# An audio encoder layer on one core: keys and queries projected transposed from folded float32 weights, score products summed by TensorE transposes, LayerNorm's scale put into the scores

## The chip, the cores and the metric

The kernel runs on one core of a Trainium2 chip. The metric is the time of one execution on the device in microseconds. The program is one launch; five engines (TensorE or PE, VectorE or DVE, ScalarE or ACT, GpSimd or POOL, and SyncE or SP, which here issues nearly all DMAs) each run their own instruction stream in the order in which it is written, and wait for one another by semaphores.

## The reference

```python
patches = x[:, idx, :].reshape(B, n, 128)          # B = 64 series, n = 10 overlapping patches
h = einsum('bnp,dp->bnd', patches, W) + b          # 640 tokens, d = 512
# attention over axis 0 of "b, s": 16 heads of 32, rotary positions, causal
q, k, v = ln(h) @ Wq.T, ln(h) @ Wk.T, ln(h) @ Wv.T
q, k = rope(q, k)
scores = q . k / sqrt(32), causal
heavy = top_k(sum over queries of softmax(scores), int(0.1 * 10))   # one key for each head
scores = where(heavy | (|i - j| <= 1), scores, -max)
h = h + (softmax(scores) . v) @ Wo.T
gate, up = split(ln(h) @ w_gate_up.T)              # 2 * 2048
h = h + (silu(gate) * up) @ w_down.T
```

`ln` is LayerNorm without weights. Each of the 64 series has 10 positions, so attention is 10 x 10 for each series and head.

## The kernel before

**Tokens.** The 640 tokens lie in five tiles of 128. A tile holds four positions of 32 series (`QUADRANTS`): tiles 0 and 1 are positions 0 to 7 of group 0 (the first 32 series), tiles 3 and 4 those of group 1, and tile 2 has positions 8 and 9 of both. Matrix products run in float32r with each operand split into a high and a low part, so each product is three matmuls (`mm3`). ACT makes the high parts; DVE or POOL the low ones, by subtraction.

**Front, group 0.** `embed` makes h for five tiles on PE; DVE takes LayerNorm's statistics, POOL the power, DVE `normalise`; PE transposes the result, and `project` makes keys, queries and values, 15 tiles of 12 matmuls. DVE turns keys and queries (`rotate`: three operations on PSUM), POOL adds the two halves (`rotation_sum`). SP writes each tile of k, q and v to a scratch tensor `regroup` in HBM (`leave`, four DMAs) and reads it back (`enter`), so that a partition holds one quarter of the heads of one series: `k_all`, `q_all`, `v_all`. Scores of query i are then one product over its i + 1 keys (`key_products`, L236) and one sum over the 32 channels of a head (L707), both on a partition's own 128 channels; POOL does some of the products (`POOL_SCORES`, `POOL_VALUES`). Softmax (`softmax_in`, `exponential` on ACT, `softmax_out`) runs twice: once to find the heavy key (`heavy_keys`), once with the mask. `value_products` (L240) multiply values by probabilities; PE sums them over keys and transposes them at once by real matmuls with an identity (`value_sums`, L1014). Then `project_out`, the second LayerNorm, and its transposes.

**First pass, tiles 0 and 1.** The feed-forward network goes over 16 blocks of weights, streamed from HBM into four slots of `stage`. For each block PE does `gate_up` (24 matmuls of 256 columns) and `down` of the block before (6 of 512); ACT does the silu and the high parts; DVE `up_product` (L847) and `low_product` (L853); POOL the low parts of the weights (`lo_gu`, `lo_down`, L364). Between the blocks' operations, in an order written out by hand, DVE does all of group 1's attention, since tiles 2 to 4 need it. PE's `value_sums` of group 1 stand after block 11, and `project_out` of tiles 2, 4 and 3 among blocks 12 to 15.

**Second pass, tiles 2 to 4.** The same 16 blocks again, 384 columns wide, with no attention beside it.

## Time and profile before

| | us |
|---|---|
| timed runs (3), median | 328.0 (327.45 to 328.83) |
| the profiled execution, its own time | 324.37 |
| its span, first to last instruction | 322.6 |
| PE busy | 278.0 |
| DVE busy | 209.8 |
| POOL busy | 157.7 |
| ACT busy | 112.0 |

Busy times are sums over stages with different limits. The profiled execution took 3.6 us less than the median of the timed runs; 1.8 us of its time lie outside the span. The granted TensorE clock was 0.973 of full speed in the mean.

### The profile page before, as it was taken

The numbers are of one execution on the slowest core, as the hardware profiler recorded it, in microseconds if no ns is written. First come the engines' busy times: TensorE is split into PE (matmuls) and PEld (weight loads), VectorE is DVE, ScalarE is ACT, GpSimd is POOL, SyncE is SP. The second block draws the span as 40 slices with busy tenths as digits, with TensorE's granted clock in tenths as the row PEclk, the third lists the DMA queues.
The fourth block names the chain that finished last, engine by engine and source line by source line (L and its number), as shares of the span: only waits on it lengthen the run. The fifth ranks groups of instructions, "written<-read, shape, count | busy, mean of one in ns | idle before, by whom it ended". The sixth has DMA issues, their size and how long they took to land.

```text
span 322.6 us, 4390 instructions
## 1 busy us (share of the span) xinstructions
PE 278.0 (86%) x1528; PEld 244.4 (76%) x1528; DVE 209.8 (65%) x307; ACT 112.0 (35%) x185; POOL 157.7 (49%) x107
## 2 busy tenths in 40 slices
PE   2989769969495799849757999899999999999994
PEld 1558648849385798749647998789999999999993
DVE  3687999999959998768499634676342333234213
ACT  4561101035101444562722223253443343344320
POOL 0565795109679598765399404542233223222310
PEclk9999989997999899998979999999999999999999
DMA  7903787504554053524320500252732442340003
GB/s 251 408 6 67 177 280 172 188 17 120 151 139 163 2 189 106 195 98 139 142 108 0 197 0 0 100 192 63 272 127 98 145 148 98 108 162 23 0 0 98
DMA packets 17902, 39.89 MB, mean 124 GB/s; under 512 B 2208, under 2 KB 10656, under 8 KB 17376
## 3 DMA queue, kind: packets, MB, share of 16 engines
q1 hardware_dynamic: 17600, 39.32, 37.8%
q10 hardware_dynamic: 288, 0.39, 0.3%
q8 instruction: 7, 0.11, 0.1%
q14 instruction: 7, 0.06, 0.1%
HBM read 34.46 MB, written 5.24 MB: 123 GB/s over the span
## 4 chain that ended last, share of the span: by engine, by line
PE 49%; DVE 28%; issue 9%; ACT 5%; POOL 3%; DMA 3%; SPq 2%; DVEq 0%; ACTq 0%; POOLq 0%
PE ps L201 41%; DVE prod L236 5%; PE ps L1014 4%; DVE hT L853 3%; DVE sm L707 3%; SPq L274 2%; POOL wvo L364 2%; DVE pr L735 2%; DVE gu L847 2%; DMA bias_raw<-b_tok 1%; DVE xn L670 1%; DVE prod L240 1%; DVE xT L677 1%; DVE rstd L667 1%; DVE rowv L725 1%
## 5 line engine op out<-in xcount | busy, mean ns | idle before, releaser
L201 PE MATMUL ps<-xT,wgu 128*128 128x256 f32 (+1 forms) x768 | 121.2, 314 | 1.9 <-DVE xT L677 1.8
L201 PEld LDWEIGHTS ps<-xT,wgu 128*128 128x128 f32 x768 | 118.1, 192 | 5.3 <-DVE xT L677 2.5
L364 POOL TENSOR_TENSOR wd<-stage,wd 128x512 fp32r<-128x512 f32 x32 | 51.6, 1613 | 80.1 <-ACT wd L477 80.1
L201 PE MATMUL ps<-wd,hT 128*128 128x512 f32 x240 | 64.0, 409 | 15.2 <-DVE hT L853 13.6
L201 PEld LDWEIGHTS ps<-wd,hT 128*128 128x128 f32 x240 | 45.3, 195 | 25.2 <-DVE hT L853 15.0
L847 DVE TENSOR_TENSOR gu<-silu,ps 128x256 f32<-128x256 f32 (+1 forms) x32 | 15.5, 484 | 62.1 <-PE ps L201 44.9
L364 POOL TENSOR_TENSOR wgu<-stage,wgu 128x1024 fp32r<-128x1024 f32 x16 | 40.1, 2505 | 12.3 <-ACT wgu L477 12.3
L477 ACT ACTIVATE wgu<-stage 128x1024 fp32r<-128x1024 f32 x32 | 33.8, 1055 | 22.1 <-PE ps L201 22.1
L853 DVE TENSOR_TENSOR hT<-gu,hT 128x256 fp32r<-128x256 f32 (+1 forms) x32 | 24.3, 759 | 19.8 <-ACT hT L477 19.8
L201 PE MATMUL ps<-wvo,xT 128*128 128x512 f32 x120 | 31.0, 412 | 5.7 <-issue 3.2
L201 PEld LDWEIGHTS ps<-wvo,xT 128*128 128x128 f32 x120 | 23.2, 197 | 11.8 <-POOL wvo L364 3.4
L1014 PE MATMUL ps<-const,prod 128*128 128x128 f32 x220 | 27.6, 287 | 5.1 <-DVE prod L240 5.1
L1014 PEld LDWEIGHTS ps<-const,prod 128*128 128x128 f32 x220 | 27.0, 202 | 6.2 <-issue 5.4
L578 ACT ACTIVATE silu<-ps 128x256 f32<-128x256 f32 (+1 forms) x32 | 13.9, 436 | 47.6 <-PE ps L201 47.6
L477 ACT ACTIVATE xT<-ps 128x512 fp32r<-128x512 f32 (+1 forms) x16 | 9.1, 571 | 53.4 <-PE ps L1014 26.7
L477 ACT ACTIVATE hT<-gu 128x256 fp32r<-128x256 f32 (+1 forms) x32 | 14.8, 462 | 35.8 <-DVE gu L847 35.7
L240 DVE TENSOR_TENSOR prod<-v_all,pr 128x896 f32<-128x896 f32 (+8 forms) x15 | 25.9, 1765 | 0.1
L477 ACT ACTIVATE wd<-stage 128x512 fp32r<-128x512 f32 x32 | 20.0, 625 | 8.5 <-PE ps L201 8.5
L236 DVE TENSOR_TENSOR prod<-q_all,k_all 128x128 f32<-128x128 f32 (+7 forms) x15 | 21.5, 1434 | 0.0
L387 POOL TENSOR_TENSOR rot<-rot_cos,rot_sin 128x512 f32<-128x512 f32 x10 | 12.8, 1284 | 17.5 <-DVE rot_sin L698 17.5
L838 DVE TENSOR_TENSOR wgu<-stage,wgu 128x1024 fp32r<-128x1024 f32 x16 | 19.7, 1234 | 1.0 <-ACT wgu L477 1.0
L707 DVE TENSOR_REDUCE sm<-prod 128x4 f32<-128x128 f32 (+9 forms) x20 | 17.5, 885 | 0.5
(76 smaller groups left out, 257.4 us busy)
## 6 DMA issues: line engine op xcount, KB each, us to landing
stage<-w_ffn SPq DMA_DIRECT2D x32, 768.0 KB, 4.3
regroup<-rot SPq DMA_DIRECT2D x40, 64.0 KB, 2.5
regroup<-v_out SPq DMA_DIRECT2D x20, 64.0 KB, 2.0
stage<-w_k SPq DMA_DIRECT2D x1, 1024.0 KB, 6.4
stage<-w_q SPq DMA_DIRECT2D x1, 1024.0 KB, 8.9
stage<-w_v SPq DMA_DIRECT2D x1, 1024.0 KB, 10.9
stage<-w_o SPq DMA_DIRECT2D x1, 1024.0 KB, 12.9
k_all<-regroup SPq DMA_DIRECT2D x4, 256.0 KB, 2.7
```

The source lines that it names most:

```text
L201: ins = pe.matmul(dst, lhs[a], rhs[b], start=first and n == 0, stop=last and n == 2)
L236: return eng.tensor_tensor(products(i), repeated(q_all[:, g, i], 1, i + 1), k_all[:, g, 0:i + 1], ALU.mult)
L240: return eng.tensor_tensor(products(i).rearrange("p j (h d) -> p j h d", d=HD), v_all[:, g, 0:i + 1].rearrange("p j (h d) -> p j h d", d=H ...
L364: pool.tensor_tensor(dst, src, f32(hi), ALU.subtract).then_inc(done, 1)
L387: pool.tensor_tensor(rot[:, n % ROT], rot_cos[:, n % 2], rot_sin[:, n % 2], ALU.add).then_inc(rot_sum, 1)
L477: act.activation(dst, src, ACT.Copy).then_inc(done, 1)
L578: act.activation(silu[:, ring, cols], ps[:, gate, at:at + P * TILES[p]], ACT.Silu).then_inc(silu_done[p], 1)
L707: dve.tensor_reduce(sm[:, i, :, 0:i + 1].rearrange("p h j -> p j h"), products(i).rearrange("p j (h d) -> p j h d", d=HD), AX_X, ALU.add). ...
L838: dve.tensor_tensor(wgu[:, ring, 1], stage[:, slot, 0:2 * KT * P], f32(wgu[:, ring, 0]), ALU.subtract)\
L847: dve.tensor_tensor(gu[:, ring, cols], silu[:, ring, cols], ps[:, up, at:at + P * TILES[p]], ALU.mult)\
L853: dve.tensor_tensor(hT[:, ring, 1, cols], gu[:, ring, cols], f32(hT[:, ring, 0, cols]), ALU.subtract).then_inc(hT_lo[p], 1)
L1014: ins = pe.matmul(dst, products(i)[:, j], cut["ident"], start=j == 0, stop=j == i)
```

## The change

**Keys and queries.** LayerNorm subtracts a mean and multiplies by one number for each token. The mean is taken out of the embedding's weights (`token_mean`, `tok_mid`), and these are multiplied with Wk and Wq on PE (`fold_matrix`, and `fold_column` for the embedding's bias). So keys and queries without LayerNorm's scale are one float32 matmul of the raw patches (`project`), and come out transposed: channels in partitions, tokens along the row. Their four chunks of 128 channels are ordered so that a rotation is between chunks. They need no trip through HBM. LayerNorm's scale of the query's and of the key's token are multiplied into the scores instead (`scales` on POOL, `scale_tables` and `scaled` on DVE).

**Scores.** `products` makes, for four positions of queries at once (128 lanes wide, two positions: 64), the products with all of 4, 8 or 10 keys, causal or not, in four operations for each `ii`. `score_sums` transposes each 128 x 128 piece on PE and adds the four chunks in PSUM, by matmuls in transpose mode; `reduced` adds the last eight of 32 channels. A partition now holds a query's position and series, and a row 3 x 16 x 10 scores. `key_totals` on PE adds the first softmax over queries and positions.

**Values.** Wv is folded likewise (`fold_matrix`, `fold_bias`, `value_tile`), the result scaled by LayerNorm's scale on ACT, and still goes through HBM, now with four DMAs of 32 partitions for `enter`. `values` multiplies two keys at a time, 1024 elements in each operation; `value_sums` sums and transposes by transpose mode. POOL does no products any more.

**Other.** 16 matmuls on constant data stand at PE's start; the output is added into `h` in place.

The core of the diff:

```diff
+            def leave(t):
+
+                sp.wait_ge(v_sb, t + 1)
                 for q, (g, i) in enumerate(QUADRANTS[t]):
...
+                    sp.dma_start(regroup[g, :, i, :], v_out[GB * q:GB * (q + 1), t % 2]).then_inc(v_gone[t % 2], 16)
+
+            def enter(g, at):
+
+                for q in range(NQ):
+                    sp.dma_start(v_all[GB * q:GB * (q + 1), at, :], regroup[g, :, at, :]).then_inc(dma_v[g], 16)
...
+            def value_in(g, t):
+                sp.wait_ge(v_gone[t % 2], 16 * NQ * (t // 2 + 1))
+                places = [i for group, i in QUADRANTS[t] if group == g]
+                enter(g, slice(places[0], places[-1] + 1))
...
+            for t in range(NT):
+                leave(t)
+                if 1 <= t <= 3:
+                    value_in(0, t - 1)
+            sp.wait_ge(fold_mm, 6)
...
+            def rotation_sum(n, pair):
+
+                g, x = PROJECT[n]
+                pool.wait_ge(rot_read, KT * n + 2 * pair + 2)
+                at = CHUNKS[2 * pair]
+                chunks = slice(at, at + 3, 2)
+                pool.tensor_tensor(kq[g][x][:, chunks], by_cos[:, chunks], by_sin[:, chunks], ALU.add).then_inc(rot_sum, 1)
...
+            for n in range(2):
+                for pair in range(2):
+                    rotation_sum(n, pair)
...
+            scales()
             for k in range(KT):
...
+                lo_wo(k)
+            for n in range(2, 4):
+                for pair in range(2):
+                    rotation_sum(n, pair)
...
             def values_out(t):
 
-                n = PROJECT.index(("v", t))
-                act.wait_ge(project_mm, n + 1)
+                act.wait_ge(value_mm, t + 1)
+                act.wait_ge(rstd_set, 1)
                 if t >= 2:
-                    act.wait_ge(v_gone[t % 2], 64 * (t // 2))
-                act.activation(v_out[:, t % 2], ps[:, PROJECT_BANK[n % len(PROJECT_BANK)], :], ACT.Copy).then_inc(v_sb, 1)
+                    act.wait_ge(v_gone[t % 2], 16 * NQ * (t // 2))
+                act.activation(v_out[:, t % 2], ps[:, VALUE_BANK[t], :], ACT.Copy, scale=h_rstd[:, t:t + 1]).then_inc(v_sb, 1)
...
+            for t in range(NT):
                 values_out(t)
             exponential(0)
+            for t in range(2):
+                act.wait_ge(v_gone[1 - t], 16 * NQ * (2 + t))
+            act.wait_ge(score_mm, len(PIECES) // 2)
+            hi_gu(A, 0, 0, 0)
             exponential(1)
             exponential(2)
-            for t in range(NT - 2, NT):
...
+            def lo_row():
+                dve.wait_ge(fold_out, 6)
+                rows = slice(BR, 2 * BR)
+                dve.tensor_tensor(fold_row[rows], ps[rows, FOLD_BANK["v", "row"], :], f32(fold_row[rows]), ALU.subtract)\
+                   .then_inc(fold_lo, 1)
...
+            def rotate(n, pair):
+
+                g, x = PROJECT[n]
+                dve.wait_ge(fold_out, 2 + 2 * "kq".index(x))
+                if n:
+                    dve.wait_ge(rot_sum, 2 * n + pair - 1)
+                for at in (2 * pair, 2 * pair + 1):
...
+                    dve.scalar_tensor_tensor(by_cos[:, c].rearrange("p (i b) -> p i b", b=GB), src, own, repeated(cos, 2, GB),
+                                             ALU.add, ALU.mult)
+                    dve.scalar_tensor_tensor(by_sin[:, (c + 2) % KT].rearrange("p (i b) -> p i b", b=GB), src, own,
+                                             repeated(sin, 2, GB), ALU.add, ALU.mult).then_inc(rot_read, 1)
...
+            def products(g, ii):
+
+                k, q = kq[g]["k"], kq[g]["q"]
+                if g:
+                    dve.wait_ge(pv_mm, 3)
+                n, at = KEYS[ii], P * ii
+                wide = WIDTH[ii] // GB
+                for place, c in enumerate(CHUNKS):
+                    dve.wait_ge(rot_sum, 4 * g + 2 + place // 2 + 1)
+                    query = q[:, c, at:at + WIDTH[ii]].rearrange("p (q b) -> p q b", b=GB)
+                    key = k[:, c, 0:GB * n].rearrange("p (j b) -> p j b", b=GB)
+                    dve.tensor_tensor(sprod[ii][:, :, c].rearrange("p j (q b) -> p j q b", b=GB),
+                                      repeated(query, 1, n), repeated(key, 2, wide), ALU.mult).then_inc(score_prod, 1)
...
+                for n, bank in enumerate(SCORE_BANK[g, ii]):
+                    dve.wait_ge(score_mm, PIECES.index((g, ii, n)) + 1)
+                    m = min(4, KEYS[ii] - 4 * n)
+                    dve.tensor_reduce(sr[0:WIDTH[ii], ii, :, 4 * n:4 * n + m].rearrange("p h j -> p j h"),
+                                      ps[0:WIDTH[ii], bank, 0:P * m].rearrange("p (j h f) -> p j h f", j=m, h=H),
+                                      AX_X, ALU.add).then_inc(score_sum, 1)
...
+                dve.wait_ge(score_sum, len(PIECES) // 2 * (g + 1))
+                step(dve.tensor_tensor(sm[:, :, :, :], sr[:, :, :, :], repeated(rr[:, g], 2, H), ALU.mult))
+                step(dve.tensor_tensor(sm[:, :, :, :], sm[:, :, :, :],
+                                       repeated(cut["causal"].rearrange("p (i j) -> p i j", j=NPOS), 2, H), ALU.min))
...
+            def heavy_keys(g):
+
+                dve.wait_ge(heavy_mm, g + 1)
+                total = ps[:, HEAVY_BANK[g], 0:H * NPOS].rearrange("p (h j) -> p h j", h=H)
+                step(dve.tensor_reduce(hvm[:, 0], total, AX_X, ALU.max))
...
+                    dve.tensor_tensor(vprod[ii][rows, j:j + PAIR].rearrange("p j (h d) -> p j h d", d=HD),
+                                      v_all[rows, j:j + PAIR].rearrange("p j (h d) -> p j h d", d=HD),
+                                      repeated(pr[rows, ii, :, j:j + PAIR].rearrange("p h j -> p j h"), 3, HD), ALU.mult)\
+                       .then_inc(pv_prod, 1)
...
+            products(0, 2)
+            lo_fold()
+            products(0, 1)
+            products(0, 0)
+            reduced(0, 2)
+            reduced(0, 1)
+            scale_tables()
+            reduced(0, 0)
             softmax_in(0)
-            rotate("k", 3)
+            lo_row()
             softmax_out(0)
-            heavy_keys()
+            rotate(2, 0)
+            heavy_keys(0)
             softmax_in(1)
             softmax_in(2)
+            rotate(2, 1)
             softmax_out(1)
-            values(0, 7, 6)
+            values(0)
             softmax_out(2)
-            values(0, 5, 4, 3, 2, 1, 0)
-            rotate("q", 3)
-            rotate("k", 4)
-            rotate("q", 4)
+            values(1)
+            values(2)
+            rotate(3, 0)
+            rotate(3, 1)
...
+            reduced(1, 2)
             first_pass(3)
-            scores(1, 9)
+            reduced(1, 1)
+            reduced(1, 0)
             first_pass(4)
             softmax_in(3)
             first_pass(5)
             up_product(A, 6, 0)
             softmax_out(3)
             low_product(A, 6, 0)
-            heavy_keys()
             first_pass(7)
+            heavy_keys(1)
...
-            values(1, 9)
+            values(3, 0, 6)
             up_product(A, 10, 0)
-            values(1, 6)
+            values(3, 6)
             low_product(A, 10, 0)
-            values(1, 5, 3)
+            values(4)
             up_product(A, 11, 1)
-            values(1, 2, 1)
             low_product(A, 11, 1)
-            values(1, 0)
+            values(5)
...
+                for k in range(KT):
+                    ins = pe.matmul(ps[:, FOLD_BANK[x, "matrix"], :], tok_mid[:, k, 0:P], weights(x, k),
+                                    start=k == 0, stop=k == KT - 1)
+                ins.then_inc(fold_mm, 1)
...
+                    dst, weight = ps[:, PROJECT_BANK[g, x][c], :], fold[x][:, P * c:P * (c + 1)]
+                    if g == 0:
...
+            def score_sums(g, ii, lasts):
+
+                pe.wait_ge(score_prod, KT * (SCORES.index((g, ii)) + 1))
+                rows = WIDTH[ii]
+                for n, bank in enumerate(SCORE_BANK[g, ii]):
+                    read_out(*lasts[n])
+                    m = min(4, KEYS[ii] - 4 * n)
+                    for j in range(m):
+                        for c in range(KT):
+                            ins = pe.matmul(ps[0:rows, bank, P * j:P * (j + 1)], sprod[ii][:, 4 * n + j, c], cut["ident"],
+                                            is_transpose=True, start=c == 0, stop=c == KT - 1)
+                    ins.then_inc(score_mm, 1)
...
+                    rows = slice(0, WIDTH[ii])
+                    ins = pe.matmul(ps[:, HEAVY_BANK[g], 0:H * NPOS], cut["batch"][rows],
+                                    pr[rows, ii].rearrange("p h j -> p (h j)"), start=ii == 0, stop=ii == NI - 1)
+                ins.then_inc(heavy_mm, 1)
...
-                    for j in range(i + 1):
-                        ins = pe.matmul(dst, products(i)[:, j], cut["ident"], start=j == 0, stop=j == i)
-                    ins.then_inc(pv_mm, 1)
+                rows, n = WIDTH[ii], KEYS[ii]
+                for j in range(n):
+                    if j % PAIR == 0:
+                        pe.wait_ge(pv_prod, VALUES.index((u, j)) + 1)
+                    for k in range(KT):
+                        ins = pe.matmul(ps[:, UNIT_BANK[u], P * k + GB * a:P * k + GB * b], vprod[ii][0:rows, j, P * k:P * (k + 1)],
+                                        cut["ident"][0:rows, 0:rows], is_transpose=True, start=j == 0 and k == 0,
+                                        stop=j == n - 1 and k == KT - 1)
+                ins.then_inc(pv_mm, 1)
...
+            score_sums(1, 2, [("unit", 2), ("rotation", ((1, "q"), 2)), ("rotation", ((1, "q"), 1))])
+            first_pass(2, 0)
+            score_sums(1, 1, [("rotation", ((1, "q"), 3)), ("score", (1, 2, 0))])
+            first_pass(3, 1)
+            score_sums(1, 0, [("score", (1, 2, 1))])
+            for i in range(4, 7):
+                first_pass(i, i % 2)
+            key_totals(1, ("score", (1, 2, 2)))
+            for i in range(7, 12):
+                first_pass(i, i % 2)
+
```

In ACT's order, at the end of group 0's front, before (`v_out<-ps` is `values_out`, `pr<-pr` an exponential, `wgu<-stage` the first block's high part, `wvo<-stage` the high part of Wo):

```order
L507 ACTIVATE v_out<-ps 128x512 x3
L512 ACTIVATE pr<-pr 128x400
L512 ACTIVATE pr<-pr 128x320
L512 ACTIVATE pr<-pr 128x80
L507 ACTIVATE v_out<-ps 128x512 x2
L477 ACTIVATE wvo<-stage 128x512 x4
L477 ACTIVATE wgu<-stage 128x1024
L477 ACTIVATE wd<-stage 128x512
```

and now, from the last embedding tile on (`fold_row<-ps` is the folded bias of the values):

```order
L451 ACTIVATE fold_v<-ps 128x512
L438 ACTIVATE v_out,h_square<-h,h_neg 128x512 x5
L429 ACTIVATE wo<-stage 128x512 x4
L451 ACTIVATE fold_row<-ps 64x512
L465 ACTIVATE v_out<-ps,h_rstd 128x512 x5
L470 ACTIVATE pr<-pr 128x480
L429 ACTIVATE wgu<-stage 128x1024
L470 ACTIVATE pr<-pr 128x320
L470 ACTIVATE pr<-pr 128x160
L429 ACTIVATE wd<-stage 128x512
```

The first exponential stood after three `values_out`; it now stands after all five, and the second one after the split of the first feed-forward block.

On DVE, around the first softmax of group 0, now (`sr` are the sums of score products, `rr` the scale table, `fold_row` the low part that `value_tile` waits for):

```order
L684 TENSOR_REDUCE sr<-ps 128x4x16
L691 TENSOR_TENSOR sm<-sr,rr 128x480
L692 TENSOR_TENSOR sm<-sm,const 128x480
L722 TENSOR_REDUCE rowv<-sm 128x48
L723 TENSOR_SCALAR rowv<-rowv 128x48
L724 SCALAR_TENSOR_TENSOR pr<-sm,rowv 128x480
L612 TENSOR_TENSOR fold_row<-ps,fold_row 32x512
L731 TENSOR_REDUCE rowv<-pr 128x48
L732 RECIPROCAL rowv<-rowv 128x48
L733 TENSOR_TENSOR pr<-pr,rowv 128x480
L660 SCALAR_TENSOR_TENSOR by_cos<-ps,column,const 128x320
L662 SCALAR_TENSOR_TENSOR by_sin<-ps,column,const 128x320
```

The low part of the folded bias (L612) stands behind the whole of the first `softmax_in`, and `softmax_out` (L731 to L733) behind that, before the rotation of group 1's keys.

On PE, in the first pass, before (`xT,wgu` is `gate_up`, `wd,hT` is `down`; rows L1051 to L1085 are a loop over ten blocks):

```order
L201 MATMUL ps<-xT,wgu 128x256 x48
L201 MATMUL ps<-wd,hT 128x512 x6
L1085 UNCONDITIONAL_BRANCH
L1085 ISA
L1051 REGISTER_ALU
L201 MATMUL ps<-xT,wgu 128x256 x24
L1064 REGISTER_ALU
L201 MATMUL ps<-wd,hT 128x512 x6
L1051 REGISTER_ALU
L201 MATMUL ps<-xT,wgu 128x256 x24
```

and now, from block 0 to the first block after the key totals (`sprod` are score products, `pr,const` is `key_totals`):

```order
L232 MATMUL ps<-wd,hT 128x512 x6
L1040 MATMUL ps<-const,sprod 64x128 x40
L232 MATMUL ps<-xT,wgu 128x256 x24
L232 MATMUL ps<-wd,hT 128x512 x6
L1040 MATMUL ps<-const,sprod 128x128 x32
L232 MATMUL ps<-xT,wgu 128x256 x24
L232 MATMUL ps<-wd,hT 128x512 x6
L1040 MATMUL ps<-const,sprod 128x128 x16
...
L232 MATMUL ps<-wd,hT 128x512 x6
L1057 MATMUL ps<-pr,const 128x160 x3
L232 MATMUL ps<-xT,wgu 128x256 x24
L232 MATMUL ps<-wd,hT 128x512 x6
```

Three stretches of transposes and one of `key_totals` have been put between the blocks; each stands ahead of a `gate_up`.

## Rows read from the trace of the kernel before

**Rows 1.** The page: the span, and busy us, share and instructions of PE.

```profile
span 322.6 us, 4390 instructions
PE 278.0 (86%) x1528; PEld 244.4 (76%) x1528; DVE 209.8 (65%) x307; ACT 112.0 (35%) x185; POOL 157.7 (49%) x107
```

**Rows 2.** Windows: stretch, length, busy us of each engine, PE clock, DMA share, GB/s.

```profile
28.00:60.80 32.80, 28.46 (x118) 22.20 (x117) 31.09 (x47) 2.99 (x5) 20.96 (x16) 0.95 0.71 190
60.80:87.50 26.70, 19.22 (x110) 16.64 (x108) 25.61 (x49) 9.41 (x16) 14.06 (x9) 0.94 0.41 113
102.50:184.40 81.90, 66.52 (x445) 61.33 (x445) 69.21 (x73) 33.23 (x55) 59.43 (x28) 0.94 0.34 119
184.40:215.60 31.20, 29.76 (x191) 25.97 (x190) 16.90 (x34) 10.04 (x19) 11.02 (x11) 1.00 0.18 65
215.60:322.60 107.00, 102.72 (x534) 95.81 (x534) 39.05 (x53) 40.61 (x64) 26.48 (x16) 1.00 0.31 105
```

**Rows 3.** The chain that ended last: start us, us, what.

```profile
174.56 10.05 PE ps L1014 x90
...
196.65 0.44 PE ps L983 x4
...
215.58 102.07 PE ps L201 x531
```

**Rows 4.** Timeline of the embedding tiles on PE, at either clock.

```profile
9.27 0.63 PE L954 MATMUL ps<-wtok,pat 128*128 128x512 f32 x1
9.69 0.63 PE L956 MATMUL ps<-wtok,pat 128*128 128x512 f32 x1
...
15.67 0.48 PE L952 MATMUL ps<-wtok,pat 128*128 128x512 f32 x1
...
16.55 0.50 PE L958 MATMUL ps<-bias,share 64*128 64x512 f32 x1
```

**Rows 5.** Timeline of PE's weight loads: the four loads of one tile's transposes.

```profile
213.13 0.42 PEld L983 LDWEIGHTS ps<-const,xn 128*128 128x128 f32 x4 [0.29 <-DVE xn L670]
```

**Rows 6.** Timeline of DVE in the first pass, and two groups by shape.

```profile
106.74 0.68 DVE L236 TENSOR_TENSOR prod<-q_all,k_all 128x512 f32<-128x512 f32 x1
107.46 0.69 DVE L707 TENSOR_REDUCE sm<-prod 128x16 f32<-128x512 f32 x1
...
108.39 0.82 DVE L236 TENSOR_TENSOR prod<-q_all,k_all 128x640 f32<-128x640 f32 x1
...
L240 DVE TENSOR_TENSOR prod<-v_all,pr 128x1024 f32<-128x1024 f32 x1 | 1.2, 1225 | 0.1
...
L698 DVE TENSOR_TENSOR rot_sin<-ps,const 128x256 f32<-128x256 f32 x20 | 7.4, 413 | 0.0
```

**Rows 7.** Timeline of SP's queue: two value tiles leave and one comes back.

```profile
70.78 1.77 SPq L274 DMA_DIRECT2D regroup<-v_out  x4
73.89 0.34 SPq L282 DMA_DIRECT2D v_all<-regroup  x1
74.27 1.89 SPq L274 DMA_DIRECT2D regroup<-v_out  x4
77.85 0.34 SPq L282 DMA_DIRECT2D v_all<-regroup  x1
```

**Rows 8.** Timeline of ACT: the first exponential, a value tile, an exponential in the first pass.

```profile
52.71 0.60 ACT L507 ACTIVATE v_out<-ps 128x512 f32<-128x512 f32 x1 [2.13 <-PE ps L201]
60.85 0.54 ACT L512 ACTIVATE pr<-pr 128x400 f32<-128x400 f32 x1 [7.54 <-DVE pr L726]
```

**Rows 9.** Timeline: a product on DVE, and POOL's operation beside it.

```profile
113.17 3.28 DVE L236 TENSOR_TENSOR prod<-q_all,k_all 128x896 f32<-128x896 f32 x1
...
112.82 2.68 POOL L364 TENSOR_TENSOR wgu<-stage,wgu 128x1024 fp32r<-128x1024 f32 x1
```

**Rows 10.** Groups by line on POOL: busy us, mean ns, idle before.

```profile
L364 POOL TENSOR_TENSOR wgu<-stage,wgu 128x1024 fp32r<-128x1024 f32 x16 | 40.1, 2505 | 12.3 <-ACT wgu L477 12.3
...
L240 POOL TENSOR_TENSOR prod<-v_all,pr 128x1152 f32<-128x1152 f32 (+3 forms) x5 | 12.9, 2586 | 0.0
...
L236 POOL TENSOR_TENSOR prod<-q_all,k_all 128x768 f32<-128x768 f32 (+2 forms) x5 | 12.7, 2561 | 2.4 <-DMA q_all<-regroup 2.4
```

782 lines of the change are left out of this document (369 added, 413 removed).

## The prediction

> **What bounds the kernel now.** I read the page, then the windows by stage, then the chain of waits and the timelines. PE is busy 278.0 of 322.6 us [rows 1], but the windows show that it is the limit in two stages only: 102.7 of 107.0 us in the second pass, and 29.8 of 31.2 us at the end of the first [rows 2]. The chain agrees: one piece of 102.07 us on PE to the end [rows 3]. The change does not touch the second pass. In the other stages DVE is the busiest: 31.1 of 32.8 us before the first softmax of group 0 is ready (28.0 to 60.8), 25.6 of 26.7 us from there to the first `low_attn` (87.5), and 69.2 of 81.9 us from the start of the first pass (102.5) to the end of group 1's value sums (184.4) [rows 2]. So the change is worth what it does to DVE's order in these three stretches, and to what DVE waits for.
>
> DVE's time in the first pass is not all its own. A product of 896 elements took 3.28 us, with POOL in an operation of 2.68 us when it came up [rows 9], where 640 elements undisturbed took 0.82 [rows 6]. A DVE operation takes about 0.15 us and 1.05 ns per element: 512 took 0.68 or 0.69, 640 took 0.82, 1024 took 1.225 [rows 6]. By that rule the stretch 102.5 to 184.4 holds 6.7 us of products (8, of 5248 elements), 8.9 of sums (10, of 7040), 5.5 of value products (7, of 4224), 24 operations of 256 elements for the blocks (0.41 each, 9.9) and some 9.4 for softmaxes, masks and heavy keys: 40.4 us. The other 28.8 of 69.2 are waits for POOL inside the operations.
>
> **The front until the first softmax is ready (60.8 now).** PE leads here. A float32 matmul goes as two instructions; 90 of 128 columns took 10.05 us [rows 3], so one takes 0.223 us, 0.89 at 512 columns and 0.56 at 320. `fold_matrix` is 4 x 0.89 = 3.6, `project` 4 x 0.56 = 2.2. `fold_column` has 16 matmuls of one column, 32 weight loads; the loads of a transposed tile come 0.1 us apart, four in 0.42 [rows 5], so at least 3.3; at most 0.3 for each of 32, 9. I take 4, near the loads. The 16 matmuls on constants and the mean end at about 8, on the low clock: 512 columns in 0.42 us there [rows 4], 1.2 GHz, so 16 x 0.45 = 7.1. Then k: 8 + 3.6 + 4 + 2.2 = 17.8, q the same: 27.6. Five embedding tiles at 1.3 us (15.67 to about 17.0 [rows 4]) 34.1, `fold_matrix` of v 37.7, copy and `lo_fold` 39.0. DVE, which has rotated and made `products(0, 2)` by 33, stands before `lo_fold`, so `products(0, 1)` (4 x 1.15, as the next starts before the last has ended) and `(0, 0)` (4 x 0.6) end at 46.1; sums 2.8, scale tables 1.4, the last sum 0.6, scaling 1.3, `softmax_in` 1.5: 53.7, with 2 us for POOL's split of Wo beside it 55.7. Term A: 55.7 - 60.8 = **-5 us** (between -10 and +5, the latter with the columns at 9 us).
>
> **The first exponential.** Now it starts at 60.85, released by its input from DVE [rows 8]. In the new order ACT does it behind `values_out(4)`, and that chain starts only when DVE has made `lo_row`, 0.7 us after `softmax_in(0)`. Call that L. Value tile and ACT's copy of 0.60 us [rows 8] end at L + 1. Four DMAs leave, issue 1.8 us; from the first issue to the next read 3.1 and 3.6 us pass [rows 7]. So tile 0 has landed at L + 4.2, `values_out(2)` ends at L + 4.9. SP has meanwhile sent tile 1 (to L + 4.6), and then issues the four new DMAs of `value_in` (0.43 each, to 6.4), then tile 2: issue to 8.2, landed 9.6. `values_out(4)` ends at 10.3, the exponential at L + 11. Behind it wait `softmax_out`, PE's key totals, the mask and everything later on DVE; nothing covers it. Before, two rotations did. Term B: 0.7 + 11 = **+12 us** (9 to 14). What is late next is the second exponential, behind `leave(4)` and the block's split: L + 18, but its input comes at L + 19, so that wait is nearly covered.
>
> **The rest of group 0 on DVE.** `softmax_out` 1.9, rotations of group 1 in 16 operations of 320 elements on PSUM at 0.4 (256 took 0.41 [rows 6], so 0.4 from start to start) 6.6, heavy keys 2.3, two masked `softmax_in` 4.0, `softmax_out` 2.4, and `values` 11 operations of 1024 elements, 12.7: 29.9, against 26.7 now [rows 2]. Term C: **+3 us** (-1 to +6). From `low_attn(0)` to the first `gate_up`, 15 us, I change nothing: the same `project_out`, LayerNorm and POOL's `lo_gu` stand there.
>
> **Group 1 in the first pass.** By the same rule DVE's own work becomes 10.9 us of products (12, of 8704 elements, since non-causal pairs are made too), 3.9 of sums, 13.4 of value products (11 x 1.225), 9.9 for the blocks and 11.3 for softmaxes of 480 elements and two scaling operations: 49.4, +9. POOL loses its products, 12.7 and 12.9 us in the whole kernel [rows 10], about 10 of the 59.4 us in this stretch [rows 2]; if the waits shrink in proportion, 28.8 becomes 24, -5. New waits: `key_totals(1)` needs `softmax_out(3)` and stands ahead of `gate_up` 7, which thereby follows it (24 x 0.112 = 2.7 us, and the totals 0.8) instead of lying beside it; `score_sums` of 32 and 16 transposes (0.1 each) stand ahead of `gate_up` 3 and 4, which DVE's next blocks need. I take +6. Term D: **+10 us**. Bounds: +4 if only the first two count; +22 if each POOL operation of the stretch meets a DVE product, which is what laying the blocks out one after another gives.
>
> At the end of the pass `value_sums(5)` has 16 transposes for 20 matmul instructions, -0.4; the rest stays.
>
> The Trainium skill ("SBUF — State Buffer", on the shared port pair) says that a DVE operation with two SBUF inputs and a GpSimd operation hold one port pair exclusively, so that the loser fully blocks. The trace agrees [rows 9]. By it alone the stretch would be set by the sum of both engines' port work; POOL's loss and DVE's gain nearly cancel, and D would be about +4.
>
> **Sum.** -5 + 12 + 3 + 10 = +20 us on the profiled execution's 324.4, so 344.4. The timed median lay 3.6 us above that execution, so 348.
>
> **Rivals.** (1) The exponential is not held: the value round trip ends sooner, or the wait is covered. Then B is 2, the rest as above: 338. Against it: the order of ACT's rows, and 3.1 us for each trip [rows 7]. (2) Faster: POOL's work, no longer doubled by products, falls into DVE's waits and reductions, and the waits inside DVE's operations in the first pass shrink from 28.8 to 5 us. Then D is 9 - 24 + 6 = -9, or -15 without new waits, and with A at its lower bound of -10 the sum is -10 + 12 + 3 - 15 = -10: 318. It decides when those waits fall under some 12 us. For it: products of 512 and 640 elements in the first pass ran undisturbed [rows 6]; against it: POOL keeps its 2.5 us of `lo_gu` for each block [rows 10], and DVE's two-input work grows. (3) The clock. Group 1's and group 0's sums are long stretches of transposes now. The windows show 0.94 in the first pass and 1.00 in the stretch with 90 real matmuls in a row [rows 2, 3]; no run here shows a long stretch of transposes. If they leave PE on the low clock, 72 transposes and the `project_out` and block behind them, 7 us at full clock, take some 6 us more in the PE-bound end, and the front 3: 357. The Trainium skill ("TensorE: Matmul & The Clock Gate", Part 4) says that transpose mode does not count as busy for the clock. That speaks for this case; the trace has only four transposes at a time.
>
> **How the numbers follow.** Likeliest: slower by about 20, terms as above, 0.55, own range 338 to 358. Rival 1 (still slower) 0.12. Rival 3 0.14. Rival 2, faster, 0.13; the small remainder lies around no change. What this measurement can tell from no change is about 0.5%, 1.6 us. Faster 0.14, same 0.04, slower 0.82. The range must leave out no more than 0.2: the faster case and a little above; 331 to 362.
>
> **What would show it.** In the changed profile: first softmax input on DVE near 56; ACT's first exponential with an idle DVE of some 11 us before `softmax_out`; first `gate_up` near 113; `project_out` of tile 2 near 204; the last stretch of PE unchanged at 102 us. I am wrong if the exponential starts within 2 us of its input, if the DVE products in the first pass run at 1.2 us with POOL busy beside them, or if the folds on PE take half of what I gave them.

## The result, and the profile after

The changed kernel took 368.8 us (median of 4 runs, 368.28 to 369.72), the one before 327.7 beside it: 1.125 times the time, interval 1.121 to 1.130. The prediction, 348 us with a range of 331 to 362, had the direction right and the size at half. The profiled execution has a span of 367.9 us against 322.6 [rows 1], 45.3 more. That is some 4 us more than the medians differ (41.0): the profiled execution of the kernel before lay 3.4 us under its median, that of the changed kernel 1.0 above. Of the runs below, executions at a lower granted clock are left out, one of ten of `all_together` (378.7 us) and two of four of `all_pieces_128` (344.6 and 340.4 us). The page of the changed kernel:

```profile
span 367.9 us, 4574 instructions
PE 301.1 (82%) x1678; PEld 259.3 (70%) x1678; DVE 206.3 (56%) x293; ACT 110.4 (30%) x189; POOL 125.9 (34%) x85
...
PEclk9887999955859699699569898999999999999999
```

DVE has fewer instructions and less busy time than before [rows 1], POOL 32 us less. PE's granted clock has digits of 5 and 6 in the front and the first pass. I cut both spans at the same five events, to see where 45.3 us went:

| from, to | before | after | grew by | predicted |
|---|---|---|---|---|
| start, first `softmax_out` | 61.99 | 75.10 | 13.1 | A + B = 7 |
| `softmax_out(0)`, `low_attn(0)` | 25.5 | 31.6 | 6.1 | C = 3 |
| `low_attn(0)`, first `gate_up` | 15.1 | 17.3 | 2.1 | 0 |
| first `gate_up`, `project_out(2)` | 81.7 | 108.3 | 26.6 | D = 10 |
| `project_out(2)`, end | 138.2 | 135.6 | -2.6 | -0.4 |

The last stage became 2.6 us shorter; 0.4 of that was in the sum, the rest is not explained. The timeline of DVE, around the first exponential:

```profile
59.42 0.66 DVE L724 SCALAR_TENSOR_TENSOR pr<-sm,rowv 128x480 f32<-128x480 f32 x1
60.11 0.68 DVE L612 TENSOR_TENSOR fold_row<-ps,fold_row 32x512 fp32r<-32x512 f32 x1
75.10 0.65 DVE L731 TENSOR_REDUCE rowv<-pr 128x48 f32<-128x480 f32 x1 [14.31 <-ACT pr L470]
```

and of ACT, which answers to [rows 8]:

```profile
62.70 0.69 ACT L465 ACTIVATE v_out<-ps,h_rstd 128x512 f32<-128x512 f32 x1 [0.63 <-PE ps L1029]
65.22 0.69 ACT L465 ACTIVATE v_out<-ps,h_rstd 128x512 f32<-128x512 f32 x1 [1.84 <-DMA regroup<-v_out]
67.11 0.69 ACT L465 ACTIVATE v_out<-ps,h_rstd 128x512 f32<-128x512 f32 x1 [1.20 <-DMA regroup<-v_out]
73.89 0.69 ACT L465 ACTIVATE v_out<-ps,h_rstd 128x512 f32<-128x512 f32 x1 [6.10 <-DMA regroup<-v_out]
74.48 0.59 ACT L470 ACTIVATE pr<-pr 128x480 f32<-128x480 f32 x1
```

The exponential's input is complete at 60.08; ACT runs it at 74.48, behind five copies, the last of which waited 6.10 us for its buffer. DVE stands 14.31 us. The clock and PE's waits in the first pass are in this timeline of PE:

```profile
149.64 3.67 PE L1040 MATMUL ps<-const,sprod 128*128 128x128 f32 x16 [3.83 <-DVE sr L684]
152.97 4.20 PE L232 MATMUL ps<-xT,wgu 128*128 128x256 f32 x24
...
160.04 3.10 PE L232 MATMUL ps<-xT,wgu 128*128 128x256 f32 x24
...
182.25 2.23 PE L1057 MATMUL ps<-pr,const 128*128 128x160 f32 x6 [5.88 <-DVE pr L733]
184.41 5.42 PE L232 MATMUL ps<-xT,wgu 128*128 128x256 f32 x24
```

Two pieces of attention work in PE's order (a piece of `score_sums(1, 1)`, and `key_totals(1)`) wait 3.83 and 5.88 us, and a block's 24 matmuls behind them take 4.20 and 5.42 us, against 3.1 at full clock.

### The profile page after: what moved, and what is told of

Its sections match the earlier page's. It is cut to its first block, busy times and chain, and to the rows that moved or that the text cites. A ratio compares the mean times of both kernels' runs of the same rounds, so it can differ in the third digit from the quotient of the medians.

```text
span 367.9 us, 4574 instructions
## 1 busy us (share of the span) xinstructions
PE 301.1 (82%) x1678; PEld 259.3 (70%) x1678; DVE 206.3 (56%) x293; ACT 110.4 (30%) x189; POOL 125.9 (34%) x85
## 4 chain that ended last, share of the span: by engine, by line
PE 59%; DVE 24%; issue 7%; ACT 4%; DMA 2%; SPq 1%; POOL 1%; ACTq 0%; DVEq 0%
PE ps L232 41%; DVE sprod L676 3%; DVE vprod L762 3%; PE ps L969 3%; PE ps L1040 3%; PE ps L1079 2%; PE ps L998 2%; PE ps L977 2%; DMA regroup<-v_out 2%; DVE pr L733 2%; DVE hT L831 2%; PE ps L1095 2%; PE ps L1057 1%; DVE sr L684 1%; SPq L266 1%
## 5 line engine op out<-in xcount | busy, mean ns | idle before, releaser
L329 POOL TENSOR_TENSOR wd<-stage,wd 128x512 fp32r<-128x512 f32 x32 | 57.1, 1786 | 85.0 <-ACT wd L429 85.0
L232 PE MATMUL ps<-wd,hT 128*128 128x512 f32 x240 | 63.7, 408 | 16.0 <-DVE hT L831 14.6
L762 DVE TENSOR_TENSOR vprod<-v_all,pr 128x1024 f32<-128x1024 f32 (+1 forms) x22 | 30.9, 1459 | 0.1
L676 DVE TENSOR_TENSOR sprod<-q,k 128x640 f32<-128x640 f32 (+2 forms) x24 | 28.8, 1263 | 0.0
L1040 PE MATMUL ps<-const,sprod 128*128 128x128 f32 (+1 forms) x176 | 22.2, 286 | 5.4 <-DVE sr L684 3.8
L1040 PEld LDWEIGHTS ps<-const,sprod 128*128 128x128 f32 (+1 forms) x176 | 20.9, 135 | 6.9 <-DVE sr L684 4.1
L232 PE MATMUL ps<-wo,xT 128*128 128x512 f32 x60 | 16.3, 428 | 11.3 <-issue 11.3
L232 PEld LDWEIGHTS ps<-wo,xT 128*128 128x128 f32 x60 | 12.3, 209 | 14.5 <-issue 11.8
L1079 PE MATMUL ps<-const,vprod 128*128 128x128 f32 (+1 forms) x176 | 18.4, 264 | 1.7 <-DVE vprod L762 1.7
L1079 PEld LDWEIGHTS ps<-const,vprod 128*128 128x128 f32 (+1 forms) x176 | 17.3, 149 | 3.5 <-issue 3.1
L429 ACT ACTIVATE xT<-ps 128x512 fp32r<-128x512 f32 (+1 forms) x11 | 6.2, 560 | 43.3 <-PE ps L1079 31.5
```

What stands on the lines that cost most here:

```text
L232: ins = pe.matmul(dst, lhs[a], rhs[b], start=first and n == 0, stop=last and n == 2)
L329: pool.tensor_tensor(dst, src, f32(hi), ALU.subtract).then_inc(done, 1)
L429: act.activation(dst, src, ACT.Copy).then_inc(done, 1)
L676: dve.tensor_tensor(sprod[ii][:, :, c].rearrange("p j (q b) -> p j q b", b=GB), repeated(query, 1, n), repeated(key, 2, wide), ALU.mult).t ...
L762: dve.tensor_tensor(vprod[ii][rows, j:j + PAIR].rearrange("p j (h d) -> p j h d", d=HD), v_all[rows, j:j + PAIR].rearrange("p j (h d) -> p ...
L1040: ins = pe.matmul(ps[0:rows, bank, P * j:P * (j + 1)], sprod[ii][:, 4 * n + j, c], cut["ident"], is_transpose=True, start=c == 0, stop=c = ...
```

## The experiments

All times are medians, each kernel measured beside the one before (327.5 to 328.0). The three kernels named `quiet` leave a part of the computation out.

| kernel | us | against what it edits |
|---|---|---|
| `exp0_first` | 365.0 | -3.8 |
| `exp_all_first` | 366.4 | -2.4 |
| `totals_later` | 361.6 | -7.2 |
| `sums_read_earlier` | 363.9 | -4.9 |
| `wide_column` | 365.1 | -3.7 |
| `four_edits` | 348.0 | -20.7 |
| `quiet_after` | 336.8 | -32.0 |
| `quiet_before` | 312.2 | -15.7 on before |
| `four_early_front` | 340.7 | -7.3 on `four_edits` |
| `four_pool_pieces` | 333.9 | -14.1 on `four_edits` |
| `quiet_four` | 322.8 | -25.3 on `four_edits` |
| `four_fillers` | 342.6 | -5.4 on `four_edits` |
| `pieces_after` | 355.9 | -12.9 |
| `pieces_before` | 317.8 | -9.7 on before |
| `all_together` | 327.8 | -40.9 |
| `all_pieces_128` | 332.3 | +4.5 on `all_together` |

**The held exponential (B).** On ACT:

```diff
+            exponential(0)
             for t in range(NT):
                 values_out(t)
-            exponential(0)
```

> The changed kernel (368.8 us) with one edit: on ACT exponential(0) stands ahead of the five values_out copies instead of behind them. Theory (the held exponential, term B): the scores' input to it is ready at 60.1 us, so it should run at about 60 and the wait of DVE of 14.3 us ahead of softmax_out(0) goes. Then the next hold shows: exponential(1) still stands behind hi_gu(A, 0), which waits for v_out's last copy, at 81.4; so I expect 3 to 6 us less, 363 to 366. Rival (the values' round trip through memory bounds it, the exponential only waits beside it): v_all's last piece lands at about 80 and the values' products start at once behind it, no more than 1 us less or nothing. A further reading: with PE's wait of 7 us at 70 gone, project(1, q) and value_sums should show a granted clock near 1.0 instead of 0.5.

It took 365.0 us (ratio 1.117, 1.107 to 1.127), in the first theory's range. The exponential runs at 59.38 and `softmax_out(0)` at 60.09, 15 us sooner, but the first `gate_up` comes at 118.79 against 124.00, only 5.2 sooner. The timeline of DVE in this kernel shows what stood behind the held exponential:

```profile
61.26 0.66 DVE L733 TENSOR_TENSOR pr<-pr,rowv 128x480 f32<-128x480 f32 x1
70.49 0.55 DVE L660 SCALAR_TENSOR_TENSOR by_cos<-ps,column,const 128x320 f32<-128x320 f32 x1 [8.57 <-PE ps L1001]
...
74.28 0.33 DVE L740 TENSOR_REDUCE hvm<-ps 128x16 f32<-128x160 f32 x1 [1.61 <-PE ps L1057]
```

DVE now waits for PE, where `project(1, k)` and `key_totals(0)` stand behind the five value tiles. In the timeline of PE in this kernel these follow one another without a gap, but slowly:

```profile
64.20 1.65 PE L232 MATMUL ps<-fold_v,pat 128*128 128x512 f32 x3
...
68.80 1.22 PE L1000 MATMUL ps<-pat_raw,fold_k 128*128 128x256 f32 x2
...
73.01 1.23 PE L1057 MATMUL ps<-pr,const 128*128 128x160 f32 x6
```

From the matmul that `lo_row` releases to the end of `project(1, k)` PE takes 13.06 us here, all busy, at a mean granted clock of 0.61, and 9.27 us at 1.00 in the changed kernel, where three matmuls of a value tile take 0.97 us. The hold was real, but it covered another one, made of PE's order and of the clock. The expected clock near 1.0 came only for a part: it was 0.84 from 70 to 80, but 0.50 from 62 to 70 and 0.55 from 80 to 90. So the second theory on ACT was tried too:

```diff
+            exponential(1)
+            exponential(2)
             for t in range(2):
                 act.wait_ge(v_gone[1 - t], 16 * NQ * (2 + t))
             act.wait_ge(score_mm, len(PIECES) // 2)
             hi_gu(A, 0, 0, 0)
-            exponential(1)
-            exponential(2)
```

> As exp0_first, and exponential(1) and exponential(2) also stand ahead of ACT's wait for v_out to have left and of hi_gu(A, 0). Theory (term B whole): everything from softmax_out(0) on moves by what heavy_keys(0) gains, about 8 us (79.4 to 71.4), until the values have not arrived: 8 to 12 us less than the changed kernel, 357 to 361, the upper end if the clock stays up as well. Rival: the arrival of the values stops it at 4 to 6 us, and the time is that of exp0_first.

366.4 us, 2.4 less than the changed kernel and no less than `exp0_first`: near the rival's total, but not for its reason. The values' products did not wait for their arrival; they start at 85.0 here and at 84.3 there. `softmax_out(1)` stands behind `rotate(2, 1)`, so an earlier exponential had nobody waiting for it. `four_early_front` edits PE's order (on top of `four_edits`, below), together with the moves on DVE and ACT that its expectation names; what each of them gave was not measured apart. On PE:

```diff
             value_tile(1, ("fold low", 1))
+            key_totals(0, ("score", (0, 0, 0)))
...
-            key_totals(0, ("score", (0, 0, 0)))
             project(1, "q", ...)
```

> four_edits (348.0 us) with the way of group 0 freed of the values' queue: on PE key_totals(0) stands behind value_tile(1) instead of behind project(1, k); on DVE heavy_keys(0) and softmax_in(1), (2) stand ahead of rotate(2, 0); on ACT exponential(1), (2) stand ahead of values_out(4). In four_edits heavy_keys(0) begins at 71.7 behind key_totals, which waits for the values and the projection ahead of it in PE's order, though the first softmax is out at 57.8. Theory (what was left of term B is PE's order): heavy_keys at about 60 and the values' products start when v_all has landed (its last pieces were issued at 69.0 and took 5.6), near 76 instead of 82: 4 to 7 us less, 341 to 344. Rival (project(1, k) and the rotations behind it bound the front): less than 2 us.

340.7 us, 7.3 less, a little more than expected. Heavy keys start at 60.6 instead of 71.7, the first value product at 75.92 instead of 81.74, without a wait for v_all, and the first `gate_up` at 110.04 instead of 116.16. In `all_together`, which has the same order, DVE waits 5.90 us ahead of its first value product for v_all's transfer (76.81): there the arrival of the values is the limit of the front.

**The two waits of PE in the first pass (D).** `key_totals(1)` behind the block instead of ahead of it:

```diff
             for i in range(4, 7):
                 first_pass(i, i % 2)
+            pe.wait_ge(gu_prod[A], 6)
+            gate_up(A, 7, 1)
             key_totals(1, ("score", (1, 2, 2)))
-            for i in range(7, 12):
+            down(A, 6, 0)
+            for i in range(8, 12):
                 first_pass(i, i % 2)
```

> The changed kernel with one edit: PE's key_totals(1) stands between gate_up(A, 7) and down(A, 6) instead of ahead of gate_up(A, 7). In the changed kernel PE waits 5.9 us ahead of key_totals(1) and then runs gate_up 7 at a granted clock of 0.53 in 5.4 us. Theory (these waits are on the path of the pass): 5 to 9 us less, 360 to 364. Rival (DVE is the bound of this stretch and the wait only moves): within 2 us of 368.8.

and DVE empties the scores' bank sooner:

```diff
             low_product(A, 1, 1)
+            reduced(1, 2)
             up_product(A, 2, 0)
             products(1, 0)
             low_product(A, 2, 0)
-            reduced(1, 2)
             first_pass(3)
```

> The changed kernel with one edit: on DVE reduced(1, 2), which empties the bank that the second piece of score_sums(1, 1) needs, stands ahead of up_product(2) and products(1, 0) instead of behind them. In the changed kernel PE waits 3.8 us there and gate_up 3 comes out at 157.3 instead of about 150. Theory (this bank's wait is part of the loss of the pass): 4 to 7 us less, 362 to 365. Rival (products on DVE bound the stretch, and what PE gains it waits for later): less than 2 us.

361.6 and 363.9 us: 7.2 and 4.9 less, both inside the first theory's range. In the timeline of PE of `totals_later` the wait has fallen to 1.74 us and the blocks beside it run at full clock:

```profile
177.20 3.22 PE L232 MATMUL ps<-xT,wgu 128*128 128x256 f32 x24
182.16 1.25 PE L1057 MATMUL ps<-pr,const 128*128 128x160 f32 x6 [1.74 <-DVE pr L733]
184.97 3.01 PE L232 MATMUL ps<-xT,wgu 128*128 128x256 f32 x24
```

In that of `sums_read_earlier` the 32 transposes of `score_sums(1, 1)` run in one piece:

```profile
144.72 3.68 PE L1040 MATMUL ps<-const,sprod 128*128 128x128 f32 x32
148.16 3.10 PE L232 MATMUL ps<-xT,wgu 128*128 128x256 f32 x24
```

**The columns and the clock (A).** In the changed kernel the fold and the projection of each of k and q stand so on PE:

```profile
12.11 3.71 PE L977 MATMUL ps<-tok_mid,stage 128*128 128x1 f32 x32
15.68 4.01 PE L998 MATMUL ps<-pat_raw,fold_k 128*128 128x320 f32 x8
...
22.96 4.25 PE L977 MATMUL ps<-tok_mid,stage 128*128 128x1 f32 x32
27.07 4.62 PE L998 MATMUL ps<-pat_raw,fold_q 128*128 128x320 f32 x8
```

`fold_column` takes what I gave it (4 us), but `project` twice the 2.2 us of my sum, and the windows show why (stretch, length, busy us, PE clock, DMA share, GB/s):

```profile
12.00:16.00 4.00, 4.00 (x34) 3.88 (x33) 0.00 (x0) 0.74 (x2) 0.14 (x1) 0.94 1.02 426
16.00:20.00 4.00, 4.00 (x10) 2.46 (x10) 2.70 (x6) 0.03 (x1) 0.71 (x1) 0.63 0.67 257
...
24.00:28.00 4.00, 4.00 (x26) 3.80 (x26) 0.00 (x0) 0.17 (x1) 0.00 (x0) 0.72 0.00 0
28.00:33.00 5.00, 5.00 (x11) 2.96 (x10) 4.22 (x9) 0.00 (x0) 1.72 (x2) 0.54 0.48 157
```

The edit lets the same 64 matmuls write 128 columns each:

```diff
-  ins = pe.matmul(ps[:, FOLD_BANK[x, "column"], c:c + 1], weights(x, k)[:, P * c:P * (c + 1)],
-                  tok_mid[:, k, P:P + 1], start=k == 0, stop=k == KT - 1)
+  ins = pe.matmul(ps[:, FOLD_BANK[x, "column"], P * c:P * (c + 1)], weights(x, k)[:, P * c:P * (c + 1)],
+                  tok_mid[:, k, P:P + 1].broadcast_to([P, P]), start=k == 0, stop=k == KT - 1)
```

> The changed kernel (368.8 us) with one edit: fold_column's matmuls read 128 copies of their one column instead of the one, so that each writes 128 columns; ACT copies every 128th. As many instructions, the same result. In the changed kernel the granted clock is 0.5 in much of the 12 us behind each fold_column, and project takes 4.0 and 4.6 us there against 2.2 at full clock. Theory (the 64 matmuls of one column each leave PE on the low clock, and term A was lost by it): project takes 2.2 us both times, the first softmax's input is ready 4 us sooner, and the time is 3 to 5 us less. Rival (the clock is low there for another reason, such as the waits, or PE is not what holds this stretch): project stays at 4 us, or it falls and the time does not move by more than 1 us.

365.1 us, 3.7 less. The timeline of PE in this kernel:

```profile
12.93 3.73 PE L977 MATMUL ps<-tok_mid,stage 128*128 128x128 f32 x32
16.50 2.32 PE L998 MATMUL ps<-pat_raw,fold_k 128*128 128x320 f32 x8
...
22.09 3.73 PE L977 MATMUL ps<-tok_mid,stage 128*128 128x128 f32 x32
25.66 2.32 PE L998 MATMUL ps<-pat_raw,fold_q 128*128 128x320 f32 x8
```

128 times the columns in the same 3.7 us, the clock is 1.00 in all windows from 12 to 33, and the first softmax's input is complete at 55.9 instead of 60.1: the 55.7 of my sum. The one-column matmuls ran at their own pace and left PE's clock at the lower level for the work behind them: 0.58 for the 3.9 us behind the first, 0.50 for the 4.0 behind the second, and not for 12 us each, as the expectation has it.

> The edits of exp0_first (-3.8 us), totals_later (-7.2), sums_read_earlier (-4.9) and wide_column together. Theory (four separate waits on one path): the gains add up to 16 us and what wide_column gives, about 349 us. Rival (behind them stands one limit, the work of DVE in the first pass): less than 12 us in sum, 357 or more.

348.0 us (1.061, 1.053 to 1.069), 20.7 less, where the four alone make 19.6: they add. 20 us against the kernel before were still missing.

For the clock in the rest of the front, matmuls without use stand in PE's waits (here one of five places):

```diff
+            filler(44, 1, ("score", (0, 1, 0)))
             project_out(1, 1, ("heavy", 0))
```

> four_edits (348.0 us) with matmuls that compute nothing of use (128 by 128 columns, float32, on the identity) put into five of PE's waits between 55 and 117 us: 12 ahead of the wait for lo_row, 28 ahead of the second half of project(1, q), 44 ahead of project_out(1), 14 and 6 around the transposes. In four_edits the granted clock is 0.5 from 57 to 70 and 0.69 and 0.80 from 82 to 117. Theory (PE's idle stretches leave it on the low clock, and the work behind them is on the path): the clock stays near 1.0 there, project(1, k) takes 2.6 us instead of 5.2, project_out x24 5.7 instead of 8.0, gate_up x48 6.3 instead of 8.3, and the time is 6 to 10 us less. Rival (the fillers themselves delay PE, or the slow stretches are covered by DVE): within 2 us.

342.6 us, 5.4 less; a little under the range. `project_out` x24 fell from 7.99 to 5.73 us, `gate_up` x48 from 8.33 to 5.96, and the first `gate_up` came 3.2 us sooner. The clock from 57 to 70 was 1.00 instead of 0.50.

**What POOL holds up (D).** POOL's subtractions for the first pass's weights are cut to one column, and PE reads the high part twice instead, so that the low parts of these weights are left out of the result:

```diff
-                low(wgu[:, slot % 2, 1], stage[:, slot, 0:2 * KT * P], wgu[:, slot % 2, 0], wgu_lo[A])
+                low(wgu[:, slot % 2, 1, 0:1], stage[:, slot, 0:1], wgu[:, slot % 2, 0, 0:1], wgu_lo[A])
```

> The changed kernel, with POOL's subtractions for the first pass's weights cut to one column each (PE reads the high part in the place of the low one, so it has the same work; the low parts of these weights are left out of the result). POOL then touches SBUF hardly at all in the first pass. Theory (DVE's two-input operations are held up by POOL's, 2.4 us in place of 0.4 for low_product, 8.6 in place of 4.9 for products(1, 1)): about 25 to 30 us of DVE time in the first pass goes, and 12 to 25 us of the time, 344 to 357. Rival (PE and the chain through ACT set the pass, DVE's time is covered): under 6 us. Read beside quiet_before: if term D rests on such contention, this kernel gains more from the quiet than the one before does; if not, the two gain alike.

> The kernel before (328 us) with the same cut of POOL's subtractions in the first pass, and the same part of the computation left out. I expect 8 to 18 us less (310 to 320): the waits for POOL inside DVE's operations were 28.8 us of the pass. If the contention in the changed kernel costs no more than here, this gains as many us as quiet_after does.

336.8 us (32.0 less, above the theory's 12 to 25) and 312.2 (15.7 less, inside the range). The timeline of DVE in the changed kernel, where `low_product` and `products(1, 1)`, `(1, 0)` stand:

```profile
130.72 2.40 DVE L831 TENSOR_TENSOR hT<-gu,hT 128x256 fp32r<-128x256 f32 x1 [0.73 <-ACT hT L429]
...
133.37 8.64 DVE L676 TENSOR_TENSOR sprod<-q,k 128x1024 f32<-128x1024 f32 x4
...
142.93 5.73 DVE L676 TENSOR_TENSOR sprod<-q,k 128x512 f32<-128x512 f32 x4
```

and the same three in `quiet_after`:

```profile
128.14 0.43 DVE L832 TENSOR_TENSOR hT<-gu,hT 128x256 fp32r<-128x256 f32 x1 [0.73 <-ACT hT L430]
...
130.05 4.63 DVE L677 TENSOR_TENSOR sprod<-q,k 128x1024 f32<-128x1024 f32 x4
...
138.62 2.52 DVE L677 TENSOR_TENSOR sprod<-q,k 128x512 f32<-128x512 f32 x4
```

Windows over the first pass, from the first `gate_up` to `project_out(2)`, here of the changed kernel and of `quiet_four` (below), in the columns of [rows 2]:

```profile
124.00:232.31 108.31, 80.15 (x520) 73.00 (x521) 78.11 (x78) 33.82 (x56) 55.22 (x24) 0.85 0.25 84
113.83:186.01 72.18, 68.84 (x521) 64.58 (x521) 46.26 (x77) 33.21 (x56) 14.62 (x24) 0.98 0.36 123
```

They give this for the kernels:

| kernel | pass, us | DVE busy | PE busy |
|---|---|---|---|
| before | 81.7 | 69.1 | 66.5 |
| `quiet_before` | 67.7 | 42.4 | 63.9 |
| `pieces_before` | 74.6 | 57.7 | 63.7 |
| after | 108.3 | 78.1 | 80.2 |
| `quiet_after` | 79.4 | 46.3 | 72.8 |
| `pieces_after` | 94.7 | 62.1 | 78.8 |
| `four_edits` | 95.0 | 76.9 | 78.4 |
| `quiet_four` | 72.2 | 46.3 | 68.8 |
| `all_together` | 80.2 | 62.4 | 71.4 |

The waits inside DVE's operations are 26.7 us before (69.1 - 42.4) and 31.8 after (78.1 - 46.3). With them gone, the pass is 14.0 us shorter before (81.7 - 67.7) and 28.9 after (108.3 - 79.4). In the changed kernel's list of waits for this stretch PE waits 14.6 us for `low_product`, 5.9 for the probabilities and 3.8 for the scores' bank, all on DVE, and none of its waits is put down to POOL: what the quiet gives comes by way of DVE.

> four_edits with POOL's subtractions of the first pass cut to one column, as in quiet_after. quiet_after gained 32 us on the changed kernel and quiet_before 15.7 on the one before. Theory (the waits inside DVE's operations and the four waits of PE and ACT are separate terms, both of which add): 348 less 27 to 32, that is 316 to 321, within 2 to 9 us of quiet_before (312.2). Rival (the quiet already covers part of what the four edits give): 322 to 330.

322.8 us: the rival's range, 25.3 less. The pass falls by 22.8 instead of 28.9 us, so some 6 us of what the quiet gave the changed kernel, the four edits had given already.

The quiet also takes work from POOL. The next edit keeps it, in pieces of 256 columns (for `wd` two pieces likewise):

```diff
-                low(wgu[:, slot % 2, 1], stage[:, slot, 0:2 * KT * P], wgu[:, slot % 2, 0], wgu_lo[A])
+                for a in range(0, 2 * KT * P, 256):
+                    b = a + 256
+                    ins = pool.tensor_tensor(wgu[:, slot % 2, 1, a:b], stage[:, slot, a:b], f32(wgu[:, slot % 2, 0, a:b]), ALU.subtract)
+                ins.then_inc(wgu_lo[A], 1)
```

> four_edits (348.0 us), with each of POOL's subtractions for the first pass's weights cut into pieces of 256 columns (four for a gate_up weight, two for a down weight), the same work in more instructions. Theory (an operation of DVE that collides waits until POOL's whole instruction has ended): low_product in the first pass falls from 2.4 us to about 1, and the time by 5 to 12 us. Rival (the two share the port element by element, or DVE is let in only when POOL has nothing left): durations and time as in four_edits within 1.5 us, or slower by the added instructions.

333.9 us (1.017, 1.010 to 1.025), 14.1 less and more than expected. The 16 `low_product` of the pass take 742 ns instead of 1025 in the mean, and the four products of 1024 elements in a row show it best, 6.23 us in place of 8.64 (in `four_edits` too):

```profile
122.53 6.23 DVE L682 TENSOR_TENSOR sprod<-q,k 128x1024 f32<-128x1024 f32 x4
```

That points to a wait for the end of POOL's running instruction. Alone, on either kernel:

> The changed kernel (368.8 us) with POOL's subtractions of the first pass cut into pieces of 256 columns, and nothing else. Theory (the hold by a whole instruction of POOL is a term of its own, whatever else waits): 11 to 17 us less, as the 14 us on four_edits: 352 to 358. Rival (it was worth 14 only where the other waits had gone): under 7 us.

> The kernel before (327.7 us) with the same pieces of POOL. The quiet was worth half as much here (15.7 us) as in the changed kernel (32). Theory (what the change added are operations of DVE that POOL holds up on the path): 4 to 8 us less, 320 to 324, well below what pieces_after gains. Rival (the hold costs both kernels alike, and term D has another cause): as many us as pieces_after, 314 to 317.

355.9 us (12.9 less) and 317.8 (9.7 less; 0.973, 0.967 to 0.980, faster than the kernel before). The first theory's range holds for the first, neither for the second: pieces help the kernel before nearly as much. In the pass alone they take off 13.6 us (108.3 to 94.7) and 7.1 (81.7 to 74.6). So the hold is not a thing of the change; the change makes more of it count.

> four_edits (348.0) with the early front (-7.3), POOL's pieces (-14.1) and the fillers (-5.4) together. If the terms are separate, 321 us, below the kernel before (327.7) and about as pieces_before; if the fillers and the early front give the same waits back, or the fillers now delay what became ready sooner, 325 to 332.

327.8 us (ratio 1.0015, 0.998 to 1.005), in the second range: the kernel before, to within what can be measured, and short of 321. The pass is 80.2 us, against 81.6 in `four_pool_pieces`. But the two front edits overlap: alone they brought the first `gate_up` 6.1 and 3.2 us forward from 116.16, together only 6.6, to 109.54, since the wait for v_all of 5.90 us has come in.

> all_together with POOL's pieces of 128 columns instead of 256. Theory (DVE waits for the end of the running instruction of POOL): half the hold again, 1 to 4 us less than all_together. Rival (POOL's fixed time for each instruction, of 8 and 4 instead of 4 and 2, makes POOL the bound): more time than all_together.

332.0 and 332.6 us: no gain, so the rival in time. But POOL was not simply the bound. The products of 1024 elements became shorter again (1316 ns in the mean for 1417), while one operation of DVE's softmax took 9.49 us (0.67 in `all_together`), with POOL in one 128-column piece after another:

```profile
168.13 0.45 DVE L739 RECIPROCAL rowv<-rowv 128x48 f32<-128x48 f32 x1
168.62 9.49 DVE L740 TENSOR_TENSOR pr<-pr,rowv 128x480 f32<-128x480 f32 x1
```

The timeline of POOL beside it:

```profile
167.58 1.72 POOL L384 TENSOR_TENSOR wd<-stage,wd 128x128 fp32r<-128x128 f32 x4
169.26 3.38 POOL L377 TENSOR_TENSOR wgu<-stage,wgu 128x128 fp32r<-128x128 f32 x8
172.60 1.69 POOL L384 TENSOR_TENSOR wd<-stage,wd 128x128 fp32r<-128x128 f32 x4
174.25 3.34 POOL L377 TENSOR_TENSOR wgu<-stage,wgu 128x128 fp32r<-128x128 f32 x8
```

From 169.26 on, 20 instructions of POOL went ahead of it, and DVE's operation ended at 178.1, half a microsecond behind the last of them. So DVE is not always let in at the next end.

## Why the prediction was half right

**Term A, -5 (measured -0.7).** The step that failed is "`project` 4 x 0.56 = 2.2", at full clock. It took 4.0 and 4.6 at the low level behind the one-column matmuls. With the clock kept up (`wide_column`) the input is complete at 55.9, where the sum had 55.7. Its other terms held: `fold_matrix` 3.70 for 3.6, `fold_column` 3.71 for 4.

**Term B, +12 (measured 13.8).** The mechanism was as predicted, the size nearly, in part by luck: the chain from `lo_row` took 14.3 us (60.79 to 75.10) where the sum had 11, and the 1.2 us that the kernel before also spends between input and `softmax_out` were not taken off. What was mis-sized is the landing of tile 2: a tile of values took 4.5 us from issue to landing, against 2.0 before. The DMA engines were 0.96 busy from 65.8 to 73.9, with the reads of v_all (5.6 us) beside the writes; that these delay the writes fits, but was not tested by itself. What I did not see is that the exponential was not alone: undoing it alone gave 5 of 14 us, since PE's `key_totals(0)` and `project(1, k)` stood behind the value tiles, at the low clock. "Nothing covers it" was right for the loss and misleading for the repair.

**Term C, +3 (measured 6.1).** DVE's own work in this stretch was 29.9 us in my sum, and the stretch took 31.6. The step that failed is the comparison with 26.7, which began at 60.8, ahead of the first exponential, whereas B ended behind it: 1.2 us counted in the wrong place. The other 1.7 are several small things: the eight pairs of rotations took 0.8 us more than the sum, a softmax product beside POOL 0.7 more, and DVE waited 0.5 for the totals. The 2.1 us ahead of the first `gate_up`, which I left at nothing, are the clock: `project_out` x24 took 7.41 us against 5.74. They are hardly the change's, though. In `quiet_before` and `pieces_before`, whose PE does the same as the kernel before up to there, it took 7.35 and 7.31; the profiled execution of the kernel before, with 5.74, is the fast one.

**Term D, +10 (measured 26.6)** is the miss. By the pairs of runs above, 14.9 us of it go with POOL's subtractions (28.9 against 14.0 us), and 11.7 remain in the quiet kernels (79.4 against 67.7): 7.2 that go in `quiet_four` (79.4 to 72.2), where the edits of PE's two waits are the ones that lie in the pass, and 4.5 beside PE's own added work (busy 68.8 against 63.9 us). Step by step:
- "+9 for DVE's own work" was too much: it went from 42.4 to 46.3, +3.9. My rule gave 40.4 and 49.4, too little before and too much after.
- "28.8 becomes 24, -5" had the wrong sign: 26.7 became 31.8. I shrank the waits with POOL's work. That fell by 4 us in the pass (59.3 to 55.2), not by 10, and the 12 products and 11 value products on DVE, all with two inputs in SBUF, meet more of what is left of it (`products(1, 1)` 8.64 us where 4.63 would do).
- "New waits: I take +6" put 3.5 us on the totals and the `gate_up` behind them, and listed the transposes as work. It left out the bank that the second piece of `score_sums(1, 1)` needs. That bank is read by `reduced(1, 2)`, which on DVE stood behind two products. The two edits gave 12.1 us, each with the clock that came back behind it. The clock has no term in the sum at all. PE's busy time in the pass is 80.2 us at 0.85, and 68.8 at 0.98 in `quiet_four` for the same matmuls, so some 11 us of it are low clock (an estimate from these two); no run gives back the clock in the pass alone.
- And the sum took the waits inside operations for time of the pass. Before, the pass lost 14.0 us with 26.7 us of them; after, 28.9 with 31.8. An argument for this, not tested by itself, is that transposes on PE now stand between DVE's products and PE's blocks, so that what holds DVE holds PE, which had gone on before. It agrees that the quiet was worth 22.8 us instead of 28.9 once two such waits were gone.

**The rivals.** Rival 1 (exponential not held) is refuted, by 14.31 us. Rival 2 needed waits inside operations below 12 us; they were 31.8. Rival 3 came nearest in time (357), by luck. The low clock took its share (3.7 us with the columns, 5.4 with the fillers, and part of what the two waits cost), but not through long stretches of transposes, and `project_out(2)` behind the last 72 took 3.00 us, as before (3.02). In windows of the changed kernel, with 88 transposes of scores and 72 of values:

```profile
42.00:48.10 6.10, 4.55 (x41) 4.25 (x39) 5.24 (x6) 5.88 (x15) 1.52 (x2) 1.00 0.00 0
48.10:53.70 5.60, 5.56 (x50) 5.43 (x50) 5.60 (x10) 0.32 (x1) 5.20 (x8) 1.00 0.01 3
223.30:229.90 6.60, 6.55 (x73) 6.22 (x72) 6.11 (x6) 1.30 (x4) 6.60 (x3) 0.97 0.34 118
```

The clock stays at 1.00 and 0.97 in them. The Trainium skill ("TensorE: Matmul & The Clock Gate", Part 4) says that transpose mode does not count as busy; this trace does not agree, at least for float32 transposes of 128 by 128 and smaller in a row.

The Trainium skill's rule on the shared port pair ("SBUF — State Buffer", "SBUF: two separate sides"), that the loser is blocked for the whole instruction of the other, was weighed and set aside with +4 for D. As a mechanism it is borne out by `four_pool_pieces`: a shorter instruction of POOL is a shorter wait. The 9.49 us in `all_pieces_128`, through 20 instructions of POOL, are more than it says. My use of it, adding both engines' port work, missed that the added DVE work is the kind that takes the pair, and that PE stood behind it.

## What to carry to other kernels

When work is moved from DVE's sums to PE's transposes, look in PE's order at what stands behind each new piece. A wait on DVE there stops the blocks too, and costs the clock on top. Price waits inside DVE's operations by the number of two-input operations that run beside POOL's and not by POOL's total, which fell here while the waits grew. And cut a long instruction of POOL that runs beside a busy DVE: pieces of 256 columns gained 9.7 to 14.1 us in three kernels here, pieces of 128 no more. When a held instruction is found, ask what stands behind the same event on the other engines, before counting the wait as the gain.

## What was not expected of the hardware

- 32 instructions of one column took 3.71 us, the same as with 128 columns (3.73), but only the former left PE on the low level: 4.01 us for the eight behind them against 2.32.
- After a wait of 2.56 us in `four_edits` the granted clock was 0.50 from 57 to 70, although PE was busy throughout (13.00 of 13.00 us). After the same wait in the changed kernel it was 1.00 from 57 to 70. The edit does not decide it: `totals_later` and `sums_read_earlier`, which are the changed kernel up to there, had 0.50 from 62 to 70. What does is open.
- Cutting POOL's instruction helps DVE only to a point: with pieces of 128 columns one DVE operation waited 8.8 us, until POOL had come to the end of 20 pieces in a row.
- The other way round, POOL loses to DVE's rows of products: one `wd` operation of POOL took 7.24 us where the mean is 1.79.
